# Attention with raw turned queries, norms applied to the scores, a 32-bit weighted sum, and row statistics ahead of the loop

## The reference, cut to what matters

```python
xn = ln(x, g_norm)
q = (xn @ Wq).reshape(b, n, HEADS, DIM_HEAD).transpose(0, 2, 1, 3)
kv = xn @ Wkv
k, v = (kv[..., :DIM_HEAD], kv[..., DIM_HEAD:])
k = jnp.concatenate([nk, k], axis=1)   # nk, nv: a null key and value in front
v = jnp.concatenate([nv, v], axis=1)
q = l2norm(q) * q_scale
k = l2norm(k) * k_scale
sim = jnp.einsum('bhid,bjd->bhij', q, k) * SCALE + attn_bias
attn = softmax(where(mask, sim, neg))
out = jnp.einsum('bhij,bjd->bhid', attn, v)
return ln(out.transpose(0, 2, 1, 3).reshape(b, n, HEADS * DIM_HEAD) @ Wout, g_out)
```

## Time and profile before

| | before |
|---|---|
| median of 3 runs | 546.78 us (544.27 to 547.57) |
| span of the profiled execution | 532.0 us |
| TensorE busy in the span | 468.7 us (88%) |
| VectorE | 359.7 us (68%) |
| ScalarE | 274.7 us (52%) |
| GpSimd | 284.7 us (54%) |
| opening, up to the projection of step 3 | 86.4 us, TensorE busy 59.5 |
| from the scores' end of step 15 to the end | 267.4 us, TensorE busy 234.7 |

### The profile page before, as it was taken

The page is one execution under the profiler, slowest core; times in us unless marked ns, Lnnn a source line. Parts: engine busy times, 40 slices in busy tenths (PEclk is TensorE's granted clock), DMA queues, the critical chain, the costliest instruction groups (busy, mean ns, idle before and its releaser), DMA issues.

```text
span 532.0 us, 11898 instructions
## 1 busy us (share of the span) xinstructions
PE 468.7 (88%) x3961; PEld 418.7 (79%) x3961; DVE 359.7 (68%) x879; ACT 274.7 (52%) x574; POOL 284.7 (54%) x343
## 2 busy tenths in 40 slices
PE   3946889999999999999999896499989489999997
PEld 1735777898999988898888785398989359898986
DVE  4784888888889888898766475757664524444522
ACT  3426666576667666566652422246565234453442
POOL 3738778897987979797830777400000633425100
PEclk9966999999999999999998998989999879999999
DMA  8370103709082641000010323265752312213011
GB/s 263 90 192 1 31 1 111 257 26 343 0 292 72 208 157 30 0 30 1 1 31 2 99 100 108 82 206 185 235 169 100 89 33 57 80 41 96 25 41 39
DMA packets 51616, 52.17 MB, mean 98 GB/s; under 512 B 6645, under 2 KB 49015, under 8 KB 51577
## 3 DMA queue, kind: packets, MB, share of 16 engines
q1 hardware_dynamic: 47956, 42.98, 25.5%
q0 software_dynamic: 3072, 8.39, 5.0%
q10 hardware_dynamic: 548, 0.28, 0.2%
HBM read 22.03 MB, written 29.62 MB: 97 GB/s over the span
## 4 chain that ended last, share of the span: by engine, by line
PE 59%; issue 8%; POOL 8%; ACT 5%; DMA 3%; DVE 3%; SPq 1%; DVEq 0%; ACTq 0%; POOLq 0%
PE bank L317 10%; PE bank L318 9%; PE bank L319 9%; POOL slot_x L579 6%; PE bank L322 5%; PE bank L323 5%; PE bank L1375 3%; PE bank L1655 3%; PE bank L1400 2%; PE bank L1339 2%; PE bank L1443 2%; ACT qT L666 2%; PE bank L1351 1%; PE bank L1388 1%; DMA slot_y<-yb 1%
## 5 line engine op out<-in xcount | busy, mean ns | idle before, releaser
L588 POOL DMA_INDIRECT yg<-slot_y,yrow x32 | 34.2, 1068 | 120.8 <-DMA slot_y<-yb 76.3
L561 POOL TENSOR_TENSOR rn<-sc,half 128x6 f32<-128x6 f32 (+1 forms) x48 | 60.6, 1277 | 7.9 <-DVE sc L1023 6.9
L1256 DVE TENSOR_TENSOR hl<-hw,hh 128x512 fp32r<-128x512 f32 x32 | 22.2, 693 | 57.1 <-ACT hw L837 57.1
L835 ACT ACTIVATE hh<-bank,late 128x512 fp32r<-128x512 f32 x32 | 22.0, 688 | 53.5 <-PE bank L1655 41.9
L317 PE MATMUL bank<-wqkv_h,xnT_h 128*128 128x384 f32 x96 | 39.1, 408 | 6.8 <-DVE sim L1004 6.8
L556 POOL TENSOR_TENSOR sim<-sim,mx 128x1040 f32<-128x1040 f32 x16 | 31.3, 1955 | 23.0 <-DVE mx L1007 23.0
L695 ACT ACTIVATE sq<-bank 128x384 f32<-128x384 f32 (+1 forms) x48 | 22.8, 475 | 40.3 <-PE bank L319 24.7
L524 POOL TENSOR_TENSOR biasm<-bias,mneg 128x1040 f32<-128x1040 f32 x16 | 35.7, 2229 | 3.7 <-DMA bias<-rel_scratch 3.7
L579 POOL DMA_INDIRECT slot_x<-xs,posi x32 | 31.4, 980 | 11.2 <-issue 9.4
L542 POOL TENSOR_TENSOR pr<-pe,rden 128x1024 f32<-128x1024 f32 x16 | 30.4, 1903 | 9.2 <-DVE rden L1044 4.5
L322 PE MATMUL bank<-wout_h,oT_h 128*128 128x256 f32 x128 | 33.6, 296 | 1.9 <-DVE oT_l L1038 1.9
(11 more groups left out here) (317 smaller groups left out, 1604.8 us busy)
## 6 DMA issues: line engine op xcount, KB each, us to landing
slot_x<-zrow SPq DMA_DIRECT2D x4, 4352.0 KB, 14.4
xq<-slot_x SPq DMA_DIRECT2D x40, 128.0 KB, 2.1
slot_y<-yb SPq DMA_DIRECT2D x20, 256.0 KB, 2.4
fstage<-in_f_W SPq DMA_DIRECT2D x4, 512.0 KB, 4.5
out<-p_all SPq DMA_DIRECT2D x8, 256.0 KB, 2.1
xs<-in_x SPq DMA_DIRECT2D x1, 1536.0 KB, 9.5
raw_out<-in_c_Wout SPq DMA_DIRECT2D x1, 1024.0 KB, 7.8
stage<-in_m_wgate SPq DMA_DIRECT2D x8, 128.0 KB, 2.1
```

What stands on the lines that cost most here:

```text
L561: e.tensor_tensor(rn[:, lo:hi], sc[:, lo:hi], half[:, lo:hi], ALU.pow).then_inc(sems['rn'], 1)
L588: e.indirect_dma_start(out=yg[:, g % 2, r, t, :], out_offset=None, in_=ydram.ap()[:, :], in_offset=bass.IndirectOffsetOnAxis(ap=yrow[:, g ...
```

## The change

It has five parts.

1. The queries leave PSUM as they are (`qc`, ScalarE copy), the squares are taken from that copy in two parts (5 heads with the key, then 12), and the copy is turned. The factor `rn` is applied to the scores as they leave PSUM (a multiplication), and bias and mask are added in a separate addition of 128 by 1040, SBUF to SBUF. The second sequence of a tile has the heads of each pair exchanged: the matmul of head r and sequence b uses the row half r xor b and the column half b of TensorE. Clamps, bias and null bias follow that exchange.
2. The weighted sum has no upper and lower parts: `pT` and the values `v_own`, `v_other` are plain 32-bit, four 64 by 64 matmuls of 512 columns. `vblk`, its zeroing, its lower parts and L1417 go; VectorE subtracts the null value as it reads PSUM.
3. On TensorE the eight matmuls of Wout with `oT_l` stand behind the turning of the queries, and the waits of the weighted sum (`before_av`) stand ahead of the third projection bank.
4. The statistics of the first norm are taken in five groups of tiles (`row_stats`, 1, 3, 4, 4 and 4 tiles) in steps -2 to 2, and finished by `norm_rows` on GpSimd.
5. The bias load is issued as three transfers for two, the null row as two for one.

The diff, cut:

```diff
-        NORM_PARTS = ((2 * QH, H + 1), (QH, 2 * QH), (0, QH))
+        NORM_PARTS = ((2 * QH, H + 1), (0, 2 * QH))
+        NN = len(NORM_PARTS)
+        X_GROUPS = ((0, 1), (1, 4), (4, 8), (8, 12), (12, NT))
...
             # SyncE
-            e.dma_start(nulls[:, :], a['nulls'].to_broadcast([P, 2 * DH + H])).then_inc(sems['ld_cols'], 16)
+            for b in range(2):
+                e.dma_start(nulls[b * S:(b + 1) * S, :], a['nulls'][b:b + 1, :].to_broadcast([S, 2 * DH + H])).then_inc(sems['ld_cols'], 16)
...
             # GpSimd
+            def norm_rows(n):
+                t0, t1 = X_GROUPS[n]
+                e.wait_ge(sems['mvx'], 2 * (n + 1))
+                e.tensor_tensor(nmx[:, t0:t1], mvx[:, t0:t1, 0], fixed[:, 1:2].to_broadcast([P, t1 - t0]), ALU.mult)
+                e.tensor_tensor(vex[:, t0:t1], mvx[:, t0:t1, 1], fixed[:, 0:1].to_broadcast([P, t1 - t0]), ALU.add).then_inc(sems['ln1_ve'], 1)
+                e.wait_ge(sems['ln1_ve'], n + 1)
+                e.tensor_tensor(rsx[:, t0:t1], vex[:, t0:t1], half[:, 0:t1 - t0], ALU.pow).then_inc(sems['ln1_rs'], 1)
+                e.wait_ge(sems['ln1_rs'], n + 1)
+                e.tensor_tensor(nbx[:, t0:t1], nmx[:, t0:t1], rsx[:, t0:t1], ALU.mult).then_inc(sems['ln1_nb'], 1)
...
             def after_first_projection():
-                e.wait_ge(sems['rn'], NB3)
-                e.wait_ge(sems['ln1_nb'], 2)
+                e.wait_ge(sems['rn'], NN)
+                norm_rows(1)
...
             def after_first_scores():
+                norm_rows(2)
...
             def mask_decay():
+                norm_rows(4)
...
             def after_second_scores():
+                norm_rows(3)
...
             def mask_bias(i):
-                e.wait_ge(sems['sim'], due(NB3 * i))
+                e.wait_ge(sems['biased'], due(i))
...
+                if live(1) and live(0):
+                    mask_bias(i + 1)
+                if live(1):
+                    e.wait_ge(sems['kn2'], due(i + 1))
+                    norms(0)
                 if live(0):
                     e.wait_ge(sems['mx'], due(i + 1))
...
                 if live(1):
-                    e.wait_ge(sems['qn'], due(NB3 * (i + 1)))
-                    for n, (lo, hi) in enumerate(NORM_PARTS):
...
+                    norms(1)
...
             # ScalarE
+                    def squares(n):
+                        lo, hi = NORM_PARTS[n]
+                        e.wait_ge(sems['qc'], due(NB3 * (i + 1) + (1, NB3)[n]))
+                        e.wait_ge(sems['ss'], due(NN * i + n + 1))
+                        e.activation(sq[:, lo:hi, :], qc[:, lo:hi, :], ACT.Square).then_inc(sems['sq'], 1)
                     for m, c in enumerate(BANKS3):
...
-                        e.activation(sq[:, QH * c:QH * c + n, :], bank[1 + c][:, 0:n * DH].rearrange('p (h d) -> p h d', d=DH), ACT.Square).then_inc(sems['sq'], 1)
+                        e.activation(qc[:, QH * c:QH * c + n, :], bank[1 + c][:, 0:n * DH].rearrange('p (h d) -> p h d', d=DH), ACT.Copy).then_inc(sems['qc'], 1)
+                        if m == 0:
+                            squares(0)
...
+                    squares(1)
...
             # VectorE
+            def row_stats(n):
+                t0, t1 = X_GROUPS[n]
+                e.wait_ge(sems[('ld_x0', 'ld_x1', 'ld_x2', 'ld_x2', 'ld_x2')[n]], 16 * 1)
...
+                if isinstance(i, int) and FIRST_I <= i < FIRST_I + len(X_GROUPS) and i < 0:
+                    row_stats(i - FIRST_I)
                 at_step(after_xn, i)
...
                     for m in range(NB3):
                         e.wait_ge(sems['sim_t'], due(NB3 * i + m + 1))
-                        e.tensor_tensor(score_part(sim, m), score_bank(m), score_part(biasm, m), ALU.add).then_inc(sems['sim'], 1)
+                        e.wait_ge(sems['rn'], due(NN * (i + 1)))
+                        e.tensor_tensor(score_part(sim, m), score_bank(m), score_norm(m), ALU.mult).then_inc(sems['sim'], 1)
+                    e.wait_ge(sems['sim'], due(NB3 * (i + 1)))
+                    e.wait_ge(sems['biasm'], due(i + 1))
+                    e.tensor_tensor(sim[:, :, :], sim[:, :, :], biasm[:, :, :], ALU.add).then_inc(sems['biased'], 1)
...
+                    if hi > H:
+                        e.tensor_scalar(sc[:, H:hi], ss[:, H:hi], 1e-24, None, ALU.max)
+                    e.tensor_scalar(sc[0:S, lo:heads], ss[0:S, lo:heads], 1e-24, None, ALU.max)
+                    for r in range(2):
+                        last = e.tensor_scalar(sc[S:P, lo + r:heads:2], ss[S:P, lo + 1 - r:heads:2], 1e-24, None, ALU.max)
...
+                if isinstance(i, int) and 0 <= i < FIRST_I + len(X_GROUPS):
+                    row_stats(i - FIRST_I)
...
             # TensorE
                 def score(r, c):
                     dst, lo = score_place(r, c)
-                    head = slice(r * DH, (r + 1) * DH)
                     for b in range(2):
+                        head = slice((r ^ b) * DH, ((r ^ b) + 1) * DH)
...
+                def before_av():
+                    e.wait_ge(sems['pT'], due(2 * i))
+                    e.wait_ge(sems['v'], due(i))
+                    e.wait_ge(sems['zn'], due(i - 1))
+                    e.wait_ge(sems['rT_l'], due(i - 2))
...
+                        if m == NB3 - 1 and live(-1):
+                            before_av()
...
-                    for b in range(2):
-                        last = split_passes(e, bank[6 + b][:, :], (vblk_h[:, 1 - par, b, :], vblk_l[:, 1 - par, b, :]), (pT_h[:, :, b * S:(b + 1) * S], pT_l[:, :, b * S:(b + 1) * S]), True, True)
...
+                    for q in range(2):
+                        rows = slice(q * S, (q + 1) * S)
+                        for b in range(2):
+                            r = q ^ b
+                            value = (v_other if r else v_own)[rows, 1 - par, :]
+                            last = e.matmul(bank[6 + b][r * DH:(r + 1) * DH, :], value, pT[rows, :, b * S:(b + 1) * S], start=True, stop=True)
```

222 lines of the change are left out of this document (99 added, 123 removed).

## The result

The changed kernel takes 576.93 us, the kernel before in the same comparison 547.17: a ratio of 1.056 (95% interval 1.053 to 1.059). The direction was forecast, the size was not: 566.8 us, a ratio of 1.037, with 577 (a ratio of 1.055) at the upper end. Executions that took over 1.5% longer than the fastest of the same kernel, at a lower granted clock, are left out of the ratios and of e6's time (e6's profile is of such a one).

The account below looks back on a forecast made before the run. TensorE was busy 14.63 of 14.90 us; afterwards the projection-to-Wout chain and rT_l wait would bound steps. Opening 4.5, first steps 5.0, steady steps 11, less 0.5, make 20; 532.0 + 20 + 14.8 = 566.8 us, range 554 to 577.

Parts of the forecast that it names:

- The removed work: TensorE in a steady step: projection 3.48 instead of 3.88 us, weighted sum 1.2 instead of 1.4; savings given back to waiting.
- The chain from projection to Wout: Copy, 12-head square, row sum, clamps and oT_l before the output projection: 4.0 us, bounds 3.6 and 4.3; step 15.1 us.
- The wait ahead of the third bank: TensorE waits for rT_l before the third projection bank: 0.4 us, 0.6 more every second step; 0.7 on average.
- The opening: Before the second projection: VectorE waits for late tokens until 13.9, first projection 4.1 us later, second projection 4.5 us later.
- steps 1 and 2: Early pipeline steps with GpSimd's norms ahead of pr: 16.4 and 18.4 us, together 34.8 against 30.80 before.
- step 3: Counted among the 12 steady steps at 15.8 us, 0.9 over the present one.
- steps 0 to 2: First pipeline steps, where statistics and norms of four tiles delay pr and its transposes: +5.0 us in all.
- the last interval: Last steps, with no projection and no square ahead of oT_l: about 0.5 us won by the shorter weighted sum.
- 14.8 us outside the span: Difference between median 546.78 and profiled span 532.0, taken as unchanged time outside the span and added back.
- Rival 2: Scores and weighted sum: unlike row halves exclude each other in one PSUM bank; 574 us, or 581 if serial; chance 0.13.
- Rival 1: Steady steps: TensorE stays the bound, 13.85 us a step; 534 or about 544 us; chances 0.05 and 0.10.
- Rival 3, the lighter part: No addition stall behind wu_l, clamps overlap, half the idle of the first steps: 558.5 us; chance 0.72 shared with main forecast.

Follow-up runs that it names:

- e6: Changed kernel with GpSimd's split of an expert weight (wu_l) behind the maximum's subtraction instead of ahead of the bias with mask: 573.2 us, ratio 1.074.
- e5: Changed kernel with both output halves and VectorE's residual addition ahead of the 12-head square and row sum: 554.3 us, ratio 1.040.
- e14: Changed kernel with one clamp instead of three, leaving out the exchange of each pair's sums: 568.7 us, ratio 1.039.
- e12: Kernel of e7 with tiles regrouped, norms of tiles 2 and 3 ahead of the first pr, and wu_l behind GpSimd's subtraction: 550.3 us, ratio 1.008.
- e4: Changed kernel with TensorE's before_av waits, rT_l's included, ahead of the last matmul of the third projection bank instead of the first: 568.5 us, ratio 1.067.
- e1: Changed kernel with statistics regrouped so that the second group needs no late token: 570.3 us, ratio 1.041.
- e8: Changed kernel, unchanged, measured again beside the kernel before: 572.1 us, ratio 1.047.
- e2: Changed kernel with GpSimd's norms of the four-tile groups behind the probabilities of steps 1, 2 and 3: 569.6 us, ratio 1.041.
- e0: Kernel before, unchanged, profiled once more: 546.44 us with a span of 544.6 us.
- e7: Changed kernel with the edits of e1, e2, e4 and e5 together: 536.1 us, ratio 1.003.

## Why the forecast was right in sign and too small

**The removed work.** Right: TensorE is busy 28.48 us in the 31.88 of two steps, 14.2 a step where the earlier trace rows have 14.6; the weighted sum takes 1.05 us (1.2 forecast), the scores 1.08 us for 60 passes from start to start (192.84 to 193.92), as before. Nothing of the saving arrives, as forecast.

**The chain from projection to Wout.** Right. From the end of the third bank (184.19) to the output projection (188.12) are 3.9 us; 4.0 were forecast, of that square 0.84, sum 0.95, clamps 0.7 where 0.5 stood. e5 and e14 show by removal that this chain is the cost.

**The wait ahead of the third bank.** Right: 0.20 and 1.01 idle against 0.4 and 1.0, and wu_l is the cause of the difference between the two (e12). From the start of the transposes of zn to the bank 0.58 and 1.39 us pass where before had 0.14, so the bank is 0.44 and 1.25 late, 0.85 on average against the 0.7 of the sum. The prediction added it to the chain, and in the unchanged kernel the two do add; e4 shows that TensorE's place for the wait is not the cause. Eleven steady steps cost 10.7 us, where 0.9 each makes 9.9.

**The opening.** Second projection 5.2 us later (4.5 forecast; e1 confirms the late tokens as 4.25 of it). VectorE's statistics start at 14.79 where 13.9 was forecast.

**The step that failed: steps 1 and 2, step 3, and the last.** For steps 0 to 2 the sum has +5.0; until the transposes of step 3 it came to 12.6 - 5.2 = 7.4. Step 0 took 18.9 us from projection to projection (42.87 to 61.81), exactly as forecast; steps 1 and 2 together took 37.2 (to 99.02) where 34.8 stood. The path through pr was right and a little shorter than forecast: 11.9 and 13.1 us from the weighted sum's start to pr's end, for 12.2 and 14.0. What was mis-sized is the projection ahead of it, 3.3 and 3.5 us in the sum, as at full clock: by start to start it took 5.3 (61.81 to 67.08, at a granted clock of 0.59) and 5.0 (80.06 to 85.04, at 0.69). Against the sum that is +3.5, and the shorter path takes back 1.2. e8 agrees in size: 4.9 us at the lower clock and 4.2 at full clock (0.4 of them idle), 37.0 for both steps. TensorE's waits for oT_l there, 2.75 and 2.27 us (1.03 and 0.87 before), aren't the loss in step 1: a wait of 2.74 for pr stands behind the first. In step 2 that for pr is down to 0.41, and in e2, without the norms, the wait for oT_l (4.44 in step 1) takes its place. No experiment isolates the clock in these steps; that the lower clock is the greater part of it is read from the rows, and why it was lower stays open.

Step 3 was counted as a steady one, +0.9: it is +2.4 here. The clamp is held up by the subtraction, and the wait for oT_l is 2.53 us instead of 1.1, which is the whole difference; in e8 the same wait is followed by the lower clock, +4.0. In the last interval the sum took off 0.5; it came to +2.1 and +0.9. In both profiles a wait for rT_l of 1.31 us stands ahead of the weighted sum there (in before 0.24 us, for pT_l), of which e6, with wu_l elsewhere, has 0.37 and an interval of 12.02; the other 1.2 go with the clock. These make 2.4 + 1.5 + 2.6 of the missing 10 us, with 0.7 from the opening and 0.8 from the steady steps; the 2 us left lie in the tail and are within what it varies by.

**Span and median.** "14.8 us outside the span" was wrong (e0): 1.8 us are outside, and the profiled execution had a tail 13 us shorter than the median one. As it was added back unchanged, the forecast's number did not suffer.

**Rivals.** Rival 2 falls: products on unlike row halves that write one bank at other partitions run side by side, 1.05 us for 8 passes of 512 columns where one after another they would take 3.3, and 18 ns a score pass, as before. The Trainium skill (TensorEngine Tiling (Array Packing), Restrictions and Gotchas) says that different row tiles cannot access one PSUM bank simultaneously; these runs differ, and the measurement decides. Rival 1's premise, that the chain and rT_l could be on time, is what e7 builds: its short step is 14.07 us, 0.2 over rival 1's 13.85, but only every second one. Rival 3, the lighter part, is excluded: the addition does stand still behind wu_l and steps 0 to 2 cost more than the +5.0, not half of it.

## What to carry to other kernels

When a row sum or another step is made longer by batching, look at what is queued behind it on its engine: here oT_l and the residual addition, not the sum itself, were what TensorE waited for, and putting them ahead gave back 10 of the 10.7 us of the steady steps. The pipeline's first steps deserve a sum of their own, in which TensorE's work is not taken at full clock without a row for it. And a small VectorE operation that starts beside a GpSimd one, both in SBUF, can't be counted at its price alone: every such clamp in the rows above lasted until the GpSimd instruction ended.

## What had not been expected of the hardware

A clamp of 12 numbers a partition, 0.17 us alone, took 1.82 (after), 1.83 (e8) and 1.60 us (e14) beside a GpSimd subtraction of 1.93 us, and two of 6 numbers 1.83 us beside wu_l (e6): the small one lasts as long as the large one still runs, with one input in SBUF. GpSimd is held up in the same way: a product of one number a partition (nb) took 1.20 instead of 0.19 us in e7 beside VectorE's addition of 1.24. A wait of TensorE can cost twice: behind waits of 2.54 us (e8, step 3) and 2.70 us (e6's long steps) the granted clock of the step is 0.91, and TensorE is busy 15.8 us in place of 14.23. It doesn't follow each time, since after's step 3 waits 2.53 us and stays at 1.00, and what decides isn't shown. And an unchanged part of 255 us can take 13 us more in another execution, with 0.82 instead of 0.91 granted over a stretch of it, so spans of two profiles are compared stage by stage.
